# A graph kernel in 8 groups: the sum of a turned block moves ahead of the next tile's mask, and ScalarE issues loads on its own DMA queue

## What is computed

```python
# x: 4096 x 256, adj: 4096 x 4096 int32 (0 or 1)
Wh = x @ W.T                                   # 4096 x 256
norms = norm(Wh, axis=1)
sim = Wh @ Wh.T / (norms * norms.T + 1e-8)     # symmetric
alpha = softmax(where((adj > 0) | eye, sim, -inf), axis=1)
x1 = layernorm(x + alpha @ Wh)

mask = adj > 0
agg = mask @ x1 / max(sum(mask, axis=1), 1)
comb = concat([x1 @ W_self + b_self, agg @ W_nb + b_nb]) @ W_comb + b_comb
out = layernorm(x1 + relu(comb))
```

## Time and profile before

| | |
|---|---|
| median of 3 runs | 867.37 us (867.26 to 870.83) |
| the profiled execution | 864.09 us |
| its span on the core | 862.30 us |
| PE busy | 836.2 us, 97% |
| DVE busy | 589.6 us, 68% |
| ACT busy | 354.6 us, 41% |
| POOL busy | 74.0 us, 9% |
| mean granted clock of PE | 0.996 of full speed |

### The profile page before, as it was taken

The page is one execution under the profiler, slowest core; times in us unless marked ns, Lnnn a source line. Parts: engine busy times, 40 slices in busy tenths (PEclk is TensorE's granted clock), DMA queues, the critical chain, the costliest instruction groups (busy, mean ns, idle before and its releaser), DMA issues.

```text
span 862.3 us, 18015 instructions
## 1 busy us (share of the span) xinstructions
PE 836.2 (97%) x6703; PEld 668.7 (78%) x6703; DVE 589.6 (68%) x1420; ACT 354.6 (41%) x577; POOL 74.0 (9%) x177
## 2 busy tenths in 40 slices
PE   8999999999999999999999999989999999999997
PEld 6867777777767677777777677768888888888886
DVE  2777887888688787888887989888445333333333
ACT  4867666665555555646546546445110000000000
POOL 2400000000000000000001101111101011100111
PEclk9999999999999999999999999999999999999999
DMA  8955666479999899999999999985303312330300
GB/s 211 242 153 171 163 175 174 126 203 225 229 220 232 241 225 233 236 253 226 239 259 223 233 246 230 247 181 220 51 8 128 117 51 85 111 114 22 116 20 19
DMA packets 202862, 147.93 MB, mean 172 GB/s; under 512 B 137505, under 2 KB 169778, under 8 KB 201746
## 3 DMA queue, kind: packets, MB, share of 16 engines
q1 hardware_dynamic: 202578, 146.33, 65.4%
q0 software_dynamic: 192, 0.41, 0.2%
HBM read 95.83 MB, written 20.99 MB: 135 GB/s over the span
## 4 chain that ended last, share of the span: by engine, by line
issue 80%; PE 10%; POOL 6%; DVE 2%; ACT 1%; POOLq 1%; DMA 0%; DVEq 0%; SPq 0%; ACTq 0%
POOL rstd L619 4%; PE ps L1294 4%; POOL var_eps L617 2%; PE ps L1384 1%; PE ps L1386 1%; PE ps L1385 1%; PE ps L1324 1%; PE ps L1326 1%; PE ps L1325 1%; ACT mask L690 1%; PE ps L1378 1%; DMA feat<-xT 0%; ACT prob_hi L685 0%; DVE feat L829 0%; DVE work L974 0%
## 5 line engine op out<-in xcount | busy, mean ns | idle before, releaser
L1384 PE MATMUL ps<-feat,prob_hi 128*128 128x257 f16 x1024 | 280.7, 274 | 14.5 <-DVE big L1079 12.5
L1386 PE MATMUL ps<-feat,prob_lo 128*128 128x257 f16 x1024 | 279.9, 273 | 0.0
L1385 PE MATMUL ps<-feat,prob_hi 128*128 128x256 f16 x1024 | 278.9, 272 | 0.0
L1554 PE MATMUL ps<-big,mgroup 128*128 128x257 f16 x992 | 219.2, 273 | 0.0
L1555 PE MATMUL ps<-big,mgroup 128*128 128x256 f16 x992 | 219.2, 273 | 0.0
L1384 PEld LDWEIGHTS ps<-feat,prob_hi 128*128 128x128 f16 x1024 | 99.9, 98 | 43.8 <-issue 18.7
L678 ACT ACTIVATE work<-ps 128x512 f32<-128x512 f32 (+2 forms) x144 | 79.9, 557 | 119.1 <-PE ps L1326 115.5
L1385 PEld LDWEIGHTS ps<-feat,prob_hi 128*128 128x128 f16 x1024 | 100.6, 98 | 24.4
L713 ACT ACTIVATE mask<-work 128x1024 fp8e4<-128x1024 f16 x84 | 86.2, 1050 | 76.6 <-DVE work L1086 76.6
L1386 PEld LDWEIGHTS ps<-feat,prob_lo 128*128 128x128 f16 x1024 | 99.7, 97 | 13.7
L1554 PEld LDWEIGHTS ps<-big,mgroup 128*128 128x128 fp8e4 x992 | 97.1, 98 | 12.1
(11 more groups left out here) (130 smaller groups left out, 959.1 us busy)
## 6 DMA issues: line engine op xcount, KB each, us to landing
adj_sb<-adjT SPq DMA_DIRECT2D x128, 512.0 KB, 4.6
mask_spill<-mask SPq DMA_DIRECT2D x128, 128.0 KB, 4.1
mgroup<-mask_spill SPq DMA_DIRECT2D x8, 2048.0 KB, 8.3
xres<-x SPq DMA_DIRECT2D x8, 512.0 KB, 5.4
out<-rows SPq DMA_DIRECT2D x32, 128.0 KB, 1.7
feat<-xT SPq DMA_DIRECT2D x7, 512.0 KB, 7.1
norm_bc<-norm_row_dram SPq DMA_DIRECT2D x7, 256.0 KB, 4.1
mgroup<-mgroup SPq DMA_TRANSPOSE x84, 4.1
```

The lines of the kernel that those rows point to most:

```text
L1384: pe.matmul(acc(D + 1), prob_hi[:, s, cols], feat_hi_of(g)[:, r, 0:D + 1], start=start, stop=False)
L1385: pe.matmul(acc(D), prob_hi[:, s, cols], feat_lo_of(g)[:, r, :], start=False, stop=False)
L1386: return pe.matmul(acc(D + 1), prob_lo[:, s, cols], feat_hi_of(g)[:, r, 0:D + 1], start=False, stop=stop)
L1554: pe.matmul(agg_ps(q, D + 1), lhsT, z_hi_of(g)[:, r, 0:D + 1], start=(jb == 0), stop=False)
```

## The change

1. DVE: `block_copied(b, 0)` now stands in the pair itself, ahead of the mask of turned tile x = 2. If another pair of the row follows, its `keep` 0 and `low` 0 (`low_part`) come ahead of that sum. The sums of blocks 1 to 3 stay where they were.
2. ACT: in rows 1 to 6 the loads of adjacency are issued by ScalarE on its own DMA queue, in `unit_kept`, between the wait for `keep` and the mask. Loads issued in `diagonal` stay on SP.
3. SP: `turn_far` for part 1 now stands ahead of the store of unit 1 instead of behind it.
4. For group 5 (`ACT_X1`) ACT makes the high halves of x1 in the pair (6, 7), as it did for groups 6 and 7 later, and DVE's pieces of that group's norm come with lag 2.

```diff
 FIRST_FAR = 1
+ACT_X1 = G - 3
...
             def pair_far(a, b):
-                k = far_before(a) + b - a - 1
                 u0 = tiles_before(a)[2] + 2 + (b - a - 1) * 4
                 for m in range(4):
                     slot = (u0 + m) % 4
-                    sync.wait_ge(kept_ready, 4 * k + m + 1)
-                    if b < G - 1:
-                        load_next(a, b + 1, m, slot)
-                    elif m < 2:
-                        load_direct(a + 1, a + 1, m, slot)
-                    elif a + 2 < G:
-                        load_next(a + 1, a + 2, m - 2, slot)
-                    if m == 0:
-                        turn_far(a, b, 0)
+                    if m < 2:
+                        turn_far(a, b, m)
                     sync.wait_ge(mask_ready, u0 + m + 1)
                     if m < 2:
                         store_direct(a, b, m, slot)
                     else:
                         store_direct(b, a, m - 2, slot)
-                    if m == 1:
-                        turn_far(a, b, 1)
...
+            def load_next_far(a, b, m, slot):
+
+                if b < G - 1:
+                    of = (a, b + 1, m) if m < 2 else (b + 1, a, m - 2)
+                elif m < 2:
+                    of = (a + 1, a + 1, m)
+                else:
+                    of = (a + 1, a + 2, m - 2)
+                if max(of) < G:
+                    to, sources, part = of
+                    act.dma_start(adj_sb[:, slot, :].rearrange("p (s i) -> p s i", s=2),
+                                  adjT_v[sources, :, 2 * part:2 * part + 2, to * GW:(to + 1) * GW]).then_inc(adj_loaded[slot], 16)
+
-            def unit_kept(u, m, count):
+            def unit_kept(a, b, u, m, count):
 
                 act.wait_ge(kept_ready, count)
+                load_next_far(a, b, m, u % 4)
                 wait(act, mask_stored[u % 4], 16 * (u // 4))
                 act.activation(mask[:, u % 4, :], kept(m), ACT.Copy, saturate=False).then_inc(mask_ready, 1)
...
-                unit_kept(u0 + 2, 2, 4 * k + 3)
-                unit_kept(u0 + 3, 3, 4 * k + 4)
+                early_x1 = a - 1 == ACT_X1
+                if early_x1:
+                    x1_head(a - 1, 0)
+                unit_kept(a, b, u0 + 2, 2, 4 * k + 3)
+                if early_x1:
+                    x1_head(a - 1, 1)
+                unit_kept(a, b, u0 + 3, 3, 4 * k + 4)
+                if early_x1:
+                    x1_head(a - 1, 2)
+                    x1_head(a - 1, 3)
...
             def split_x1(a, q):
                 dve.wait_ge(rows_ready, a * GB + q + 1)
-                if a < G - 2:
+                if a < ACT_X1:
...
             def norm_work(a):
...
-                lag = 1 if a < G - 2 else 2
+                lag = 1 if a < ACT_X1 else 2
...
                     if a and far(a - 1):
-                        block_copied(G - 1, j, t0 - GB + j)
-                        if j == 0:
+                        if j:
+                            block_copied(G - 1, j, t0 - GB + j)
+                        else:
                             dve.wait_ge(prob_lo_ready, t0)
...
                 for r in range(GB):
-                    if r % 2 == 0:
-                        keep_unit(r // 2)
-                    damping(a, b * GB + r, c0 + r, f0 + r, r)
-                    low(r)
-                    if n:
-                        block_copied(b - 1, r, t0 - GB + r)
+                    if r == 2:
+                        keep_unit(a, b, 1)
+                    if r or n == 0:
+                        if r == 0:
+                            keep_unit(a, b, 0)
+                        low_part(a, b, r)
+                        if n:
+                            block_copied(b - 1, r, t0 - GB + r)
...
                 for x in range(GB):
+                    if x == 2:
+                        if b < G - 1:
+                            keep_unit(a, b + 1, 0)
+                            low_part(a, b + 1, 0)
+                        block_copied(b, 0, t0 + GB)
                     dve.wait_ge(far_loaded[x // 2], 32 * (k + 1))
                     masked_parts(t0 + GB + x, x, kept_block(x), halved(far_turned[:, 0, x]), halved(far_turned[:, 1, x]), halved)
```

More of the change, by code:

```diff
@@ L707, in diagonal, with x1_head @@
                         unit_mask(u % 4, j - 1, 16 * (u // 4))
-            def unit_kept(u, m, count):
+            def x1_head(a, q):
+                act.wait_ge(rows_ready, a * GB + q + 1)
+                act.activation(x1_hi_of(a)[:, q, :], x1_of(a)[:, q, :], ACT.Copy, scale=NORM_SCALE).then_inc(x1_hi_ready, 1)
+            def load_next_far(a, b, m, slot):
[10 more added lines that the diff above has]
+            def unit_kept(a, b, u, m, count):
                 act.wait_ge(kept_ready, count)
+                load_next_far(a, b, m, u % 4)
                 wait(act, mask_stored[u % 4], 16 * (u // 4))
@@ L734, in pair_far @@
                     if r in (1, 2):
-                        unit_kept(u0 + r - 1, r - 1, 4 * k + r)
-                unit_kept(u0 + 2, 2, 4 * k + 3)
-                unit_kept(u0 + 3, 3, 4 * k + 4)
+                        unit_kept(a, b, u0 + r - 1, r - 1, 4 * k + r)
+                early_x1 = a - 1 == ACT_X1
[8 more added lines that the diff above has]
+                    x1_head(a - 1, 3)
             def split_high(g):
@@ L1092, in masked_parts, with keep_unit, low_part @@
                 dve.tensor_tensor(shaped(prob_lo[:, s, :]), adj, low, ALU.mult).then_inc(prob_lo_ready, 1)
+            def keep_unit(a, b, m):
+                n = b - a - 1
+                t0, _, u0 = (first + more for first, more in zip(tiles_before(a), (GB + n * STEP_TILES, 0, 2 + n * 4)))
+                if n:
+                    keep(u0 + m, m, t0 - STEP_TILES + 2 * (m + 1) if m < 2 else t0, u0 + m - 3)
+                else:
+                    keep(u0 + m, m, t0, u0 - 1 + m // 2)
+            def low_part(a, b, r):
+                n = b - a - 1
+                t0, f0, _ = (first + more for first, more in zip(tiles_before(a), (GB + n * STEP_TILES, GB + n * GB, 0)))
+                damping(a, b * GB + r, scores_before(a) + GB + n * GB + r, f0 + r, r)
+                dve.wait_ge(far_hi_ready, GB * (far_before(a) + n) + r + 1)
+                dve.wait_ge(prob_lo_ready, t0 - STEP_TILES + r + 1 if n else t0)
+                dve.scalar_tensor_tensor(out=far_parts[:, 1, r, :], in0=expo[:, r, :], scalar=PROB_SCALE, in1=far_parts[:, 0, r, :],
+                                         op0=ALU.mult, op1=ALU.subtract).then_inc(far_lo_ready, 1)
             def pair_far(a, b, between):
                 n = b - a - 1
-                t0, f0, u0 = (first + more for first, more in zip(tiles_before(a), (GB + n * STEP_TILES, GB + n * GB, 2 + n * 4)))
-                c0 = scores_before(a) + GB + n * GB
+                t0 = tiles_before(a)[0] + GB + n * STEP_TILES
                 k = far_before(a) + n
@@ L1106, in beside @@
                             between.pop(0)()
-                def keep_unit(m):
-                    if n:
-                        keep(u0 + m, m, t0 - STEP_TILES + 2 * (m + 1) if m < 2 else t0, u0 + m - 3)
-                    else:
-                        keep(u0 + m, m, t0, u0 - 1 + m // 2)
-                def low(r):
-                    dve.wait_ge(far_hi_ready, GB * k + r + 1)
-                    dve.wait_ge(prob_lo_ready, t0 - STEP_TILES + r + 1 if n else t0)
-                    dve.scalar_tensor_tensor(out=far_parts[:, 1, r, :], in0=expo[:, r, :], scalar=PROB_SCALE, in1=far_parts[:, 0, r, :],
-                                             op0=ALU.mult, op1=ALU.subtract).then_inc(far_lo_ready, 1)
-                for r in range(GB):
-                    if r % 2 == 0:
-                        keep_unit(r // 2)
-                    damping(a, b * GB + r, c0 + r, f0 + r, r)
-                    low(r)
-                    if n:
-                        block_copied(b - 1, r, t0 - GB + r)
+                for r in range(GB):
+                    if r == 2:
[4 more added lines that the diff above has]
+                        low_part(a, b, r)
+                        if n:
+                            block_copied(b - 1, r, t0 - GB + r)
                     dve.wait_ge(kept_ready, 4 * k + r // 2 + 1)
@@ L1132, in pair_far @@
                     beside()
-                keep_unit(2)
-                keep_unit(3)
+                keep_unit(a, b, 2)
+                keep_unit(a, b, 3)
                 beside()
```

5 lines of the change are left out of this document (1 added, 4 removed).

## The result

The changed kernel takes **885.81 us** (median of 4 runs, 879.87 to 888.21), the kernel before beside it 867.54 (867.26 to 870.83): 1.0192 times, 95% interval 1.0134 to 1.0249. It is slower, by 18 us between the medians, where 12 us less were predicted. The profiled execution took 879.87 us, with a span of 878.1 against 862.3 of before.

The account below looks back on a forecast made before the run. The prediction took PE as the bound, waiting in rows 1 to 6 almost only for block_copied (12.5 us). Its terms -4.2 - 4.0 - 3.7 = -11.9 us brought the median from 867.37 to 855.5 us, range 852 to 867.

Parts of the forecast that it names:

- Waits inside rows: PE's waits for block_copied before tile 2, in row 1 (3.3 us) and inside later rows (0.9), go: -4.2 us.
- the slack of 2.5 us ahead of block 2: Tile 2's mask is ready about 1.3 us after block 0 ends, and PE comes at 3.9: about 2.5 us spare.
- Ends of rows: At the ends of rows 1, 2, 4 and 5, each PE wait shrinks by 1.0 us: -4.0 of 5.8 us.
- End of row 6: Block 3 starts at 579.2 instead of 582.87, with x1 high halves on ScalarE and no clock drop: -3.7 us.
- Loads on ScalarE: Each load costs ScalarE 0.44 us, but its loop with DVE takes 15.1 against PE's 15.7: cost 0.
- Rival 1: Loads on ScalarE wait 1.0 us each while SP issues transposes; time 865.1 us; chance 0.20.
- The transposes: On SP, part 1 ahead of the store of unit 1: landing time of the transposes taken as unchanged.
- The second loop: From one low 3 to the next through the transposes: 15.7 us in row 1, 13.8 in later rows.
- rival 2: Loads get in front of the transposes; with part 1 landing 3.5 us later, 10.0 us slower, 877.4; chance 0.12.
- my bounds of -2.8 to +5.6: Limits in us for how much the landing of the transposes could change, from shorter to longer.
- Rival 3: PE's waits before tile 2 stay since low 0 comes late from ScalarE; gain -7.7, time 859.7 us; chance 0.13.

Follow-up runs that it names:

- experiment 11: The kernel before with the sum's move and four high halves of x1 on ScalarE, loads and SyncE's order as before: 851.10 us, 0.9882 times before.
- Experiment 5: The changed kernel with ScalarE's loads cut to the first eighth of their columns, the rest not loaded: 850.66 us, 0.9869 times before.
- experiment 3: The changed kernel with the loads back on SyncE and part 1 of the transposes ahead of load 1: 853.58 us, 0.9859 times before.
- experiment 8: The changed kernel with only loads 2 and 3 of each pair on ScalarE, loads 0 and 1 on SyncE behind part 1: 862.38 us, 1.0004 times before.
- experiment 4: The changed kernel with loads 2 and 3 of a pair issued by ScalarE behind high part 1 of the next pair: 927.99 us, 1.0733 times before.

## Why the prediction was wrong

**Waits inside rows, -4.2: right, a little small.** In the sum's move alone row 1 fell from 81.7 to 77.6 us and rows 1 to 5 together from 237.4 to 231.6, 5.8. The wait for `block_copied` went, and the slack of 2.5 us ahead of block 2 held.

**Ends of rows, -4.0: right.** 134.7 to 131.3 us, -3.4, in the sum's move alone.

**End of row 6, -3.7: right.** The tail went from 295.6 to 291.8 in the changed kernel, -3.8, of which 1.4 is the x1 part (1.3 foreseen); in the sum's move alone it went to 293.1, -2.5. The granted clock was 1.00 in 577 to 600 and in 587 to 610 us, not 0.93 as in the earlier trace rows; this row ends some 20 us later here.

In the sum's move alone these terms, 5.8 + 3.4 + 2.5, make with 0.7 us at the start the 12.5 us between the spans (862.3 to 849.8; each is rounded). With the x1 part (experiment 11, span 848.3) it is 14.0, where the sum of the prediction was 11.9.

**Loads on ScalarE, 0: right as to ScalarE.** An issue took 0.375 us as median, not 0.44:

```profile
L715 ACTq DMA_DIRECT2D adj_sb<-adjT x82: 374/375/1337, 190.1 to 583.7; - x82
```

Experiment 5 has all these issues and goes at PE's pace. **Rival 1** falls with it: at 232.07 the load took 0.37 us in the middle of SP's 2.76 us of issuing part 1; the next, at 232.67, took 0.68. Of the 82 loads 60 were issued while SP issued transposes; they took 0.375 us as median and 0.44 as mean, the other 22 0.374 and 0.38. That is 0.06 us a load where the rival had 1.0. So the lock of the descriptor generator, of which "Perfetto Trace Analysis" of the Trainium skill tells (section "DMA Instruction — HWDGE (DVE, Sync)"), did not hold a load up for the length of a transpose's issue here.

**The transposes, "I take no change": this step failed.** The second loop of the prediction was 0.8 + 1.3 + landing + 7.7. The three small terms hold: in the handover above 0.76 from `low` 3 to the issue, 1.3 for the first transpose's issue, and 246.56 - 238.90 = 7.66 from tile 2 to the next `low` 3. The landing was 7.1 us instead of 5.9 in row 1, 16.8 us a pair; and in row 2, where I had put the median 4.1 and so 13.8 us a pair, the second transpose took 8.2, and it went from 340.61 to 358.53, 17.9 us. That is the mechanism of **rival 2**, with the change inside my bounds of -2.8 to +5.6, and I gave it 0.12. Both signs that I had named for it came: part 1 landing at 7 us and more, and PE waiting for `prob_lo` before tile 2. Its price, 10 us over before, was low (16 us between the two profiled executions, 18 and 19 between the medians), and its distribution wrong: it had most of the loss in row 1, where the loop was tightest. Measured against the sum's move alone, row 1 lost 4.3 us, row 2 8.1, rows 3 to 5 1.6, 4.3 and 1.9, the ends 7.1. The median of 4.1 for the later rows wasn't the error: in row 2 of the kernel before the second transpose of part 1 landed after 4.0 to 4.7 us, and in the changed kernel after 5.6 to 8.2 (medians 4.1 and 7.8; in row 1 5.2 and 7.0). It was to add nothing to it. I asked only how long part 1 waits for what lies ahead of it. On one queue loads 2 and 3 behind it don't matter (experiment 3); on two, what goes out after it lies beside it (experiment 8, and the 573 packets).

What would have told: the DMA share of 0.95 and 1.05 in rows 1 and 2 of the kernel before, shown above, which is not among the rows that I argued from. At that share the second queue brought no bytes sooner (232 and 214 GB/s against 241 and 231 with one queue); it only took the transposes' turn. The page that I cited, "DMA: Bandwidth & Descriptors" of the Trainium skill, says in "Issuing engines are not separate DMA queues" that DMAs of different engines "interleave with each other". I took from it that the gain is nil and not that the interleaving is a cost. The packets of the changed kernel agree with the sentence; the size of the cost is this case's.

**Rival 3** didn't occur: the wait before tile 2 for `block_copied` is 1.3 us in all.

## What to carry over

Before a transfer is put on a second queue, read the DMA share of the stretch. Where it was near full here, one queue was also an order of priority: the short transfer that the engines waited for went ahead of the bulk, and the second queue gave that up. And when a change has two parts, price them under each other: here the part that wins 14 us hid, in the sum of the whole, a part that loses more than twice that.

## What the runs showed of the hardware

- Transposes landed in 3.6 us as median with the 512 KB loads in their own queue, three of a pair's four behind part 1, and in 5.6 with the same loads in another (220 to 285 us), at the same DMA share of 0.95 to 0.96. The longest was 13.5 us (experiment 4).
- DMAs of two queues shared the DMA engines packet by packet: 573 load packets ran while the two transposes of a part 1 were under way, against 36 with one queue, and the transposes' own packets took 18 ns as median in both.
- The loss is far from proportional to the bytes on the second queue: about 0 for an eighth, 3 us for a half, 30 for all; and the two halves of the loads cost 5 and 12 us apart. How much of that bend is the DMA engines and how much the cover of PE's pace stays open. Nor was another kind of transfer tried on the second queue, or the transposes on it instead of the loads.
- 49 of ScalarE's 82 loads were issued wholly within the time in which SyncE issued one transpose, with a median of 0.375 us; in the one handover shown of experiment 3 the first load behind part 1 on SyncE's own queue took 1.91 us.
- The sum's move took 851.88 us on one chip and, with the x1 part, 851.10 on another, with runs 1.6 us apart at most; the kernel before had medians from 861.6 to 867.5 from one set of runs to the next, and runs up to 7.0 us apart within one. Why it varies more isn't shown.
